# A 128x1 memset on GpSimd behind every indirect gather of a three-layer graph kernel

## The reference

```
x = layernorm(x + L0(x))        # L0: msg = relu((x[src] * weight) @ W_msg + b_msg)
                                #     agg = segment_sum(msg, dst); relu(agg @ W_out + b_out)
x = layernorm(x + L1(L1(x)))    # each L1: xt = einsum('nd,rde->rne', x, W)   (8 relations)
                                #     msg = xt[rel, src]; agg = segment_sum(msg, dst)
                                #     relu(agg + x @ SW + b)
```

## Time and profile before

| | |
|---|---|
| median of three runs | 7131.54 us |
| profiled execution, first to last instruction (its span) | 7175.4 us |
| POOL busy | 4562.2 us (64%), 4835 instructions |
| DVE busy | 2671.7 us (37%) |
| PE / PEld busy | 2668.5 us (37%) / 2091.2 us (29%) |
| ACT busy | 606.3 us (8%) |
| DMA, queue of the gathers | 154112 packets, 315.93 MB, 17.0% of 16 engines |
| first gather starts / last gather starts | 10.06 us / 7147.39 us |

### The profile page before, as it was taken

One profiled execution on the slowest core, in us unless ns is written; L12 is line 12 of the kernel. 1 busy time (PEld: TensorE's weight loads), 2 busy tenths in 40 slices (PEclk: granted clock), 3 DMA queues, 4 the chain that ended last, 5 costly groups with the idle time before them and its releaser, 6 DMA issues.

```text
span 7175.4 us, 45352 instructions
## 1 busy us (share of the span) xinstructions
PE 2668.5 (37%) x11892; PEld 2091.2 (29%) x11892; DVE 2671.7 (37%) x5892; ACT 606.3 (8%) x1334; POOL 4562.2 (64%) x4835
## 2 busy tenths in 40 slices
PE   4334344433444343444444444443223223222223
PEld 4333333322333322223332333332222222222222
DVE  3776666666555532333332222232111111111112
ACT  2111111111111110000000000000000000000000
POOL 4666666666666646666666666665666666666665
PEclk9666666666666656666666666665555555555556
DMA  5122222222222212222222222221111111111111
GB/s 144 43 78 74 71 73 72 73 74 71 73 74 72 74 55 61 70 68 70 69 69 69 68 67 67 69 70 57 52 52 52 52 53 51 52 52 51 52 51 49
DMA packets 265749, 468.98 MB, mean 65 GB/s; under 512 B 102461, under 2 KB 155365, under 8 KB 265477
## 3 DMA queue, kind: packets, MB, share of 16 engines
q0 software_dynamic: 154112, 315.93, 17.0%
q1 hardware_dynamic: 110212, 149.64, 6.1%
q10 hardware_dynamic: 1152, 0.39, 0.0%
HBM read 343.56 MB, written 122.05 MB: 65 GB/s over the span
## 4 chain that ended last, share of the span: by engine, by line
another core or an unknown queue 48%; DVE 22%; issue 17%; PE 10%; DVEq 2%; ACT 1%; DMA 0%; SPq 0%; POOL 0%; ACTq 0%; POOLq 0%
PE bank L791 6%; DVE rows L769 5%; PE bank L1031 3%; DVE picked L1070 2%; DVE work L751 2%; DVE place L1081 2%; DVE onehot L751 2%; DVE tab L1091 1%; DVEq L776 1%; DVE agg L781 1%; DVE bank L1385 1%; DVE work L1386 1%; DVE bank L1383 1%; DVE work L1390 1%
## 5 line engine op out<-in xcount | busy, mean ns | idle before, releaser
L688 POOL DMA_INDIRECT rows<-rel_table,rel_index x3152 | 2980.9, 946 | 1643.4 <-issue 939.0
L688 POOL DMA_INDIRECT rows<-msg_table,msg_index x1600 | 1514.0, 946 | 918.9 <-issue 466.9
L791 PE MATMUL bank<-work,rows 128*128 128x128 f32 x6304 | 1188.1, 336 | 1300.7 <-issue 1282.2
L781 DVE TENSOR_TENSOR agg<-agg,bank 128x128 f32 x602 | 171.2, 284 | 3803.2 <-remote 3486.7
L791 PEld LDWEIGHTS bank<-work,rows 128*128 128x128 f32 x6304 | 1084.7, 249 | 1438.0 <-issue 1419.9
L791 PE MATMUL bank<-onehot,rows 128*128 128x128 f32 x3328 | 624.5, 361 | 890.6 <-ACT rows L657 498.8
L791 PEld LDWEIGHTS bank<-onehot,rows 128*128 128x128 f32 x3328 | 583.4, 268 | 960.3 <-ACT rows L657 524.1
L1031 PE MATMUL bank<-wr,feat 128*128 128x512 f32 x784 | 598.5, 907 | 693.1 <-issue 429.7
L751 DVE TENSOR_TENSOR work<-bank,place 128x1024 f32<-128x1024 f32 x394 | 477.1, 1212 | 7.3 <-ACT agg L956 3.8
L1031 PEld LDWEIGHTS bank<-wr,feat 128*128 128x128 f32 x784 | 207.2, 293 | 898.8 <-issue 619.6
L1020 PE MATMUL bank<-ident,sums 128*128 128x128 f32 x98 | 38.1, 389 | 1055.3 <-ACT sums L994 842.8
(11 more groups left out here) (126 smaller groups left out, 1437.0 us busy)
## 6 DMA issues: line engine op xcount, KB each, us to landing
rel_table<-tab SPq DMA_DIRECT2D x196, 512.0 KB
rows<-rel_table,rel_index POOLq DMA_INDIRECT x3152
rows<-msg_table,msg_index POOLq DMA_INDIRECT x1600
x_dram<-normed SPq DMA_DIRECT2D x98, 64.0 KB
xin<-x_dram SPq DMA_DIRECT2D x98, 64.0 KB
xin<-in_x_dram SPq DMA_DIRECT2D x97, 64.0 KB
out_dram<-normed SPq DMA_DIRECT2D x97, 64.0 KB
tab<-in_x_dram SPq DMA_DIRECT2D x24, 256.0 KB
```

What stands on the lines that cost most here:

```text
L688: nc.gpsimd.indirect_dma_start(rows[:, u, t, :], None, table, bass.IndirectOffsetOnAxis(ap=table_index[:, g, t:t + 1], axis=0)).then_inc(e ...
L781: nc.vector.tensor_tensor(out=window, in0=window, in1=sum_of(layer, st), op=ALU.add).then_inc(sems.added, 1)
L791: ins = nc.tensor.matmul(total, tile, hot[:, t, :], start=t == 0, stop=t == TPG - 1)
```

## The change

A column `dot` of 128x1 float32 is added in SBUF, and a semaphore `s_dot`. Behind each indirect gather, in all three layers and in the early gathers, POOL sets the column to zero. Each memset first waits for the one before it, which writes the same column, and increments `s_dot`. Nothing reads the column.

```diff
         eps = sb("eps", [P, 1])
+        dot = sb("dot", [P, 1])
@@
         s_pads = sem("s_pads")
+        s_dot = sem("s_dot")
@@
+        dots = [0]
+
+        def pool_dot():
+
+            need(nc.gpsimd, s_dot, dots[0])
+            nc.gpsimd.memset(dot[:, :], 0.0).then_inc(s_dot, 1)
+            dots[0] += 1
+
         def static_gather(layer, g):
@@
                     bass.IndirectOffsetOnAxis(ap=table_index[:, g, t:t + 1], axis=0)
                 ).then_inc(edge_main.rows[u][t // HALF], 16)
+                pool_dot()
```

## The result

On the chip where both kernels were timed together the changed kernel takes 7151.49 us (median of 6 runs, 7149.85 to 7155.12) and the kernel before 7131.14 us (6 runs): a ratio of 1.003, with an interval of 1.0019 to 1.0041. The forecast was 6700 us. Repeated on another chip, the kernel before took 6100.07 us and the changed one 6101.64: a ratio of 1.0003 (0.9994 to 1.0012).

A forecast was written before the change was run, and what follows sets the result against it. Bound by POOL's 10 us beat per group plus standstills forced by PE's backlog. 7175.4 + 481.6 for memsets - 915.2 of waits = 6741.8 us, times 0.9939, rounded to 6700 us; range 6300 to 7680 us.

The forecast's parts named there:

- POOL's account: POOL's span: gathers 4556.8 us, issue 1425.2, remote 807.5, PE 241.1, table stores 107.7; together 7138.3 of 7175.4 us.
- I take 0.10 us ... all of it on POOL's line: Memset behind each of 4816 gathers on POOL: 0.10 us each, +481.6 us in all; ends 0 and +1974.6 us.
- PE needs the time in which POOL makes no gathers ... the ring waits go: Waits at group borders: memsets give PE 0.8 us a group, so 915.2 of 1048.6 us of POOL's waits go.
- The standstill is all or nothing: POOL's stops at full buffers exist only if PE is a whole ring behind, so the upper end, 915.2 us, was taken.
- The added wait, cost 0: Each memset's wait for the one before: the earlier one is finished after a 0.946 us gather, so cost 0.
- B: Memset hidden in POOL's 0.30 us gap, frees nothing: beat 1.25 us, 7131 us; chance 0.09 including no memset between gathers.
- A: PE stays as late as now: POOL's waits stay and the memsets come on top, 7610 us; chance 0.34.
- D: Memset hidden in POOL's gap and PE freed, so the ring waits go: 6220 us; chance 0.03.
- C: Each memset costs POOL a dispatch gap too, 0.41 us, with all ring waits gone: 8180 us; chance 0.08.
- The factor of 0.9939: Whole kernel: median of runs 7131.5 us lies 0.61% under the profiled span 7175.4; used to scale 6741.8 to 6701 us.
- What would show it: Signs: gather starts 1.35 us apart, POOL's border waits under 150 us, no 2.8 us PE stretches, DVE's wait far below 3486.7.
- The last sign, the adds behind the last gather: End of kernel: forecast wrong if DVE's adds still trail by eight groups, a last add 20 us after the last gather.

The follow-up runs named there:

- experiments 9 to 12: On a third chip, beside the kernel before (6100.07 us): its copy 6100.19 us, the changed kernel 6101.64, the kernel before with 64-row gathers 5892.94, with 256 B rows 6099.84.
- experiment 1: Changed kernel with memsets writing 256 columns in turn, each waiting only for the one 256 before: 7201.65 us, ratio 1.002 to the kernel before.

## Why the prediction was wrong, step by step

- **POOL's account** held: 946 ns, a gap of 0.30, a beat of 1.25 us, ring waits at group borders.
- **"I take 0.10 us ... all of it on POOL's line"** failed. The term of +481.6 us measured nothing: 1.5 us where POOL alone decides. The row it rested on the earlier trace rows gave the memset's duration rightly (0.115 here). Wrong was to add it to a beat that holds an idle 0.30 us: the forecast took the gap for dispatch in line, and it is, in part, time in which POOL can do something else. Its width is read from the wider memsets, whose beat was 1.335 us at 0.220 and 1.428 at 0.315: starts are 1.113 to 1.115 us plus the memset apart, so by this line some 0.13 us are free (1.249 less 1.115); no width between 0.118 and 0.220 us was run.
- **"PE needs the time in which POOL makes no gathers ... the ring waits go"** failed, and it is the larger error: 915.2 us were to go, 41.8 went. With 6 of 8 matmuls gone the ring was as full, and with a memset of 0.22 us behind each gather half of the standstill stayed. The premise, that gathers issued back to back make PE late, failed too: on the chip of experiments 9 to 12 the same gathers at the same 1.25 us leave PE on time. Behind the lateness in the earlier trace rows is a limit of about 1.43 us a gather on some chips; between stops POOL runs over it, at each stop the backlog drains. The number stood in the trace: the distance of the gathers' starts, waits included. Two terms that lie on both sides of such a limit can't be added.
- **"The standstill is all or nothing"** failed with it. It shrinks as POOL's own beat comes near the limit: 1162.6 us at a beat of 1.203, 1048.6 at 1.249, 529.3 at 1.335, 49.2 at 1.444.
- **The added wait, cost 0**: right, by experiment 1. The 249.7 us of idleness that stand at the memset do not come from it: without the wait they move to the gathers. What the forecast did not have is that an added instruction on POOL is itself held up where PE is late (284 us inside the groups against 24 before), which the standstills at the borders then give back.
- **The rivals.** B (7131 us: hidden in the gap, frees nothing) is the mechanism measured, and it had the least thought: it had 0.09 with the case that no memset is there. A had the waits right and the price wrong, D the price right and the waits wrong, C both wrong. The sign is slower by 0.3%, just over the 0.2% that B was given.
- **The range** of 6300 to 7680 us held 7151.49 by luck: it was stretched upwards to take in A, and no case of weight lay near 7150. The cases were built from sums in which the memset, the standstill or both moved in full.
- **The factor of 0.9939** from span to median stands for a difference between executions of one kernel, not between a span and a time: where both are known, they differ by 1.7 us (7148.8 and 7150.54). It is larger than the change's effect.

**What would show it**, by the forecast's own signs: starts 1.25 us apart (B or D), waits of 1006.8 us, of which 685.1 at the gathers (A or B), PE loads still 2.8 us apart in places, DVE's `remote` 3244.1 us. Together they name B. The last sign, the adds behind the last gather, fell between: that gather starts at 7127.30 and the last add at 7141.83, 14.5 us later, where it was 21.1 before, and seven groups still trailed:

```profile
7127.30 0.94 POOL L698 DMA_INDIRECT rows<-rel_table,rel_index  x1 [0.19 <-issue]
...
7141.83 0.29 DVE L792 TENSOR_TENSOR agg<-agg,bank 128x128 f32 x1 [1.00 <-PE bank L802]
```

## What to carry to other kernels

Where an engine is idle for a fixed short time behind each instruction, test whether that gap takes work before adding a new instruction's duration to the beat. Where an engine alternates between an even beat and standstills on a full ring, compute the mean distance with the waits in it. If it is above the engine's own beat, is nearly the same in every stage, and stays when the beat is changed, there is a rate limit behind the engine, and neither faster nor slightly slower issue will move it. A gain seen on one chip (0.9904 for the wide memset) can be a loss on the next (1.1409 for nearly the same one): repeat on another before keeping it.

## What the runs showed of the hardware that was not expected

- The same kernel took 7131 (first comparison), 7183, 6097, 6100 and 7125 us in five sets of runs, each on one chip; within a set the kernel before spread by 0.4% at most. In the traces of the two sets near 6100 us nothing is late.
- A gather of 64 rows keeps POOL busy for 0.900 us, one of 128 rows for 0.944, one of 128 half rows for 0.944: nearly all of it is a fixed price per gather.
- Lateness comes in steps: in the kernel before, of the distances between PE's loads on `rows` that lie from 0.6 to 3.1 us, 249 are near 0.7 us, 178 near 1.4, 161 near 2.1 and 224 near 2.8, and only 121 elsewhere. In the changed kernel a memset on POOL started 0.9 us after its turn.
- A trace can lack records without saying so: 22,922 semaphore updates on a chip where PE is late, 98,836 for the same kernel where it is not. A wait called `remote` or `issue` there need not be what it seems.
